# Two-layer decoder on one core: ScalarE copies the last turned group of each half in stages 1 and 3, and the row statistics move to the ends of halves

## What is computed

```python
x = x + _L0_attn_ref(_layernorm(x), qk, ov)                       # one causal head
x = x + _L0_xattn_ref(_layernorm(x), ctx, ctx, mask, Wq, bq, ...) # 16 heads of 16, mask, softmax
x = x + _L0_ffn_ref(_layernorm(x), w_router, b_router, w1, ...)   # relu FFN, top 4 of 16 blocks
x = x + _L1_attn_ref(_layernorm(x), w_qkv, b_qkv, w_o, b_o)       # 16 heads of 16, adds its input
x = x + _L1_xattn_ref(_layernorm(x), ctx, ctx, itok, ...)         # 16 heads, windows of 64, rotary
x = x + _L1_ffn_ref(_layernorm(x), gate_weight, w_gate, ...)      # top 2 of 8 experts + shared
```

## Time and profile before

| | us |
|---|---|
| median of 3 runs | 920.52 (920.5 to 922.61) |
| the profiled execution | 918.35 |
| its span, first to last instruction | 916.4 |
| TensorE matmuls busy | 858.8 (94%) |
| VectorE busy | 540.7 (59%) |
| ScalarE busy | 418.9 (46%) |
| GpSimd busy | 234.0 (26%) |

### The profile page before, as it was taken

One profiled execution on the slowest core, in us unless ns is written; L12 is line 12 of the kernel. 1 busy time (PEld: TensorE's weight loads), 2 busy tenths in 40 slices (PEclk: granted clock), 3 DMA queues, 4 the chain that ended last, 5 costly groups with the idle time before them and its releaser, 6 DMA issues.

```text
span 916.4 us, 16762 instructions
## 1 busy us (share of the span) xinstructions
PE 858.8 (94%) x6400; PEld 702.6 (77%) x6400; DVE 540.7 (59%) x1363; ACT 418.9 (46%) x1218; POOL 234.0 (26%) x352
## 2 busy tenths in 40 slices
PE   4889999997999999999999999999989999999998
PEld 3777777665888788777777777777758888888887
DVE  3565767777333321577777766666655555555554
ACT  1345566565322223566665567666674212222211
POOL 2112112221232112223232656666500000000000
PEclk9999999999999999999999999999989999999999
DMA  9700000000000000000000100000000000000000
GB/s 338 302 1 19 19 13 13 13 24 5 20 12 24 12 12 11 2 2 1 1 2 1 59 13 13 22 15 2 2 1 1 12 1 13 12 13 12 12 13 11
DMA packets 10909, 24.61 MB, mean 27 GB/s; under 512 B 1488, under 2 KB 5840, under 8 KB 9680
## 3 DMA queue, kind: packets, MB, share of 16 engines
q1 hardware_dynamic: 10832, 23.55, 7.1%
HBM read 21.45 MB, written 2.10 MB: 26 GB/s over the span
## 4 chain that ended last, share of the span: by engine, by line
PE 77%; ACT 10%; DVE 10%; issue 1%; DMA 1%; SPq 0%; POOL 0%; DVEq 0%; POOLq 0%; ACTq 0%
PE sc L556 15%; PE pj L293 9%; PE pj L286 7%; ACT pr L1115 7%; PE ov L455 6%; PE pj L379 6%; PE sc L442 6%; PE sc L368 6%; PE ov L566 4%; PE pj L566 4%; PE ov L390 3%; PE pj L280 3%; PE sc L363 3%; DVE pT L792 2%; PE ov L293 2%; DVE xn L736 1%
## 5 line engine op out<-in xcount | busy, mean ns | idle before, releaser
L1115 ACT ACTIVATE pr<-sc,mx 128x128 f32<-128x128 f32 x768 | 216.7, 414 | 116.9 <-DVE mx L785 116.9
L785 DVE TENSOR_REDUCE mx<-sc 128x4 f32<-128x512 f32 x192 | 119.2, 683 | 56.5 <-PE sc L368 56.5
L379 PE MATMUL pj<-idn,pr 128*128 128x128 f32 x768 | 120.9, 281 | 20.8 <-ACT pr L1115 13.2
L792 DVE COPY pT<-pj 128x512 f32<-128x512 f32 x160 | 109.5, 686 | 33.5 <-PE pj L379 31.8
L379 PEld LDWEIGHTS pj<-idn,pr 128*128 128x128 f32 x768 | 88.1, 142 | 49.6 <-issue 20.4
L1257 POOL TENSOR_SCALAR ve<-mv 128x2 f32<-128x2 f32 x40 | 8.9, 221 | 377.1 <-DVE mv L731 377.1
L1153 ACT ACTIVATE sh<-sc 128x256 f32<-128x256 f32 x80 | 30.7, 384 | 155.6 <-PE sc L556 155.6
L1133 ACT ACTIVATE hT<-sc,vecs 128x256 f32<-128x256 f32 x64 | 30.4, 475 | 95.4 <-PE sc L442 95.4
L556 PE MATMUL sc<-xnT,W 128*128 128x256 f32 x256 | 66.4, 382 | 0.0
L556 PE MATMUL sc<-xnT,Wup 128*128 128x256 f32 x256 | 65.7, 379 | 0.0
L442 PE MATMUL sc<-xnT,W 128*128 128x256 f32 x256 | 64.1, 380 | 0.0
(11 more groups left out here) (170 smaller groups left out, 1550.0 us busy)
## 6 DMA issues: line engine op xcount, KB each, us to landing
cT<-in_ctxT SPq DMA_DIRECT2D x16, 256.0 KB, 3.1
W<-in_w SPq DMA_DIRECT2D x2, 1024.0 KB, 13.6
cT<-in_ctx SPq DMA_DIRECT2D x8, 256.0 KB, 2.7
out_x<-X SPq DMA_DIRECT2D x8, 256.0 KB, 2.0
X<-in_x SPq DMA_DIRECT2D x1, 1792.0 KB, 8.1
rws<-in_rows SPq DMA_DIRECT2D x1, 1064.0 KB, 12.0
hT<-in_tokk SPq DMA_DIRECT2D x1, 1024.0 KB, 10.4
Wx<-in_w_x SPq DMA_DIRECT2D x1, 1024.0 KB, 16.4
```

Source lines behind the costliest of these rows:

```text
L379: last = tr(bank[b][:, i * S:(i + 1) * S], pr[n % 4][:, i, :], idn[:])
L785: v.tensor_reduce(mx[n % 4][:], four(b), AX.X, ALU.max, negate=True).then_inc(mx_done, 1)
L792: v.tensor_copy(pT[n % 4][:], four(b)).then_inc(drained[b], 1)
L1115: last = a(pr[n % 4][:, i, :], bank[b][:, i * S:(i + 1) * S], ACT.Exp, bias=mx[n % 4][:, i:i + 1])
```

## The change

Four things are edited. `ACT_TURNS` gives groups 3 and 7 of stages 1 and 3 to ScalarE. On VectorE `alone0` and `alone1` go to the end of their half, behind `part1` and `part3`; `alone0` now holds `x_norm(U + 2)`, `alone1` holds `x_stats(U + 3)`, one half earlier than `x_stats(U + 2)` at the start of the next unit, so the loops begin at -3. The router's choice and the experts' weights go from `alone1` to `part2`. GpSimd's `x_inverse(U + 2)` goes from `part1` to the head of `part0`. TensorE's list of instructions is the same.

```diff
-        ACT_TURNS = {1: (), 3: (), 4: (1, 3, 5, 7)}
+        ACT_TURNS = {1: (3, 7), 3: (3, 7), 4: (1, 3, 5, 7)}
...
                 dense(U, 2 * j)
-                if f not in ATT:
-                    (alone0, alone1)[j](U)
                 (part0, part2)[j](U)
                 if f in ATT:
                     copy_probs(U, 4 * j)
-                    (alone0, alone1)[j](U)
                 dense(U, 2 * j + 1)
                 (part1, part3)[j](U)
+                (alone0, alone1)[j](U)
...
+                if stage(U + 1) == 2:
+                    router_choice(U + 1)
+                if stage(U + 1) == 5:
+                    weights(U + 1)
...
             def alone0(U):
-                if stage(U + 2) is not None:
-                    x_stats(U + 2)
+                if stage(U + 2) in (0, 1, 2, 3, 5):
+                    x_norm(U + 2)
                 if stage(U) == 2:
                     ctx_stats(U % PAIRS)
...
             def alone1(U):
-                if stage(U + 2) in (0, 1, 2, 3, 5):
-                    x_norm(U + 2)
-                if stage(U + 1) == 2:
-                    router_choice(U + 1)
-                if stage(U + 1) == 5:
-                    weights(U + 1)
+                if stage(U + 3) is not None:
+                    x_stats(U + 3)
...
             def part0(U):
+                if stage(U + 2) is not None:
+                    x_inverse(U + 2)
...
             def part1(U):
                 if stage(U + 1) == 4:
                     rotate(U + 1, 0)
-                if stage(U + 2) is not None:
-                    x_inverse(U + 2)
...
-            for U in range(-2, UNITS + 2):
+            for U in range(-3, UNITS + 2):
```

## The result

The changed kernel takes 911.9 us (median; 908.83 to 913.04 over 4 runs) against 920.82 beside it (920.5 to 922.61). The ratio is 0.9894, with a 95% interval of 0.9867 to 0.9921: about 1% faster (the ratio is estimated from all runs of both, not from the two medians). 912.2 had been forecast. The profiled execution took 911.74, with a span of 909.9 us; before it was 918.35 with 916.4.

The account below looks back on a forecast made before the run. TensorE, 77% of the last chain, was taken as the bound, so only holes in its work could be won. Terms 3.6 + 0.6 + 2.2 + 2.8 + 0.8 + 0.2 - 1.9 = 8.3 us gave a 912.2 us median, range 908.5 to 917.5.

Parts of the forecast that it names:

- (f): Stage 2, units of fold and center: statistics delay the residual TensorE waits for, 0.94 us each, a loss of 1.9 us.
- (c): ScalarE's 32 copies fit where it idles: 0 us, bound 0 to 0.1 per copy, up to 3.
- (g): Start: xn of pair 2 escapes GpSimd's memsets, 2.2 us, plus 0.6 of clock: 2.8 us, bounds 1.0 and 3.6.
- (a): Second halves of stage 1: x_norm leaves between copies 4 and 5, 3.6 us; first unit of stage 3, 0.6 us.
- (b): First halves of stages 1 and 3: statistics leave, x_norm at the end is hidden: no gain or loss.
- (d): Second halves end with statistics of three units ahead, 0.94 us, hidden: 0 us, thinnest cover 0.27 us in stage 3.
- (e): Stage 4: without statistics ahead of it the value step starts some 0.27 us earlier, eight times: 2.2 us.
- (h): Last unit of stage 1: copy 5 no longer behind x_norm and router's choice, 0.8 us; end of stage 4, 0.2 us.
- given back: Many-head stages: ScalarE's exponentials set the unit's pace, so freed time is lost; 919.2 us, no change; 12%.
- The slower one: Second halves of stages 1, 3, 4: statistics in front of the maxima delay the chain, 932.9 us in full; 6%.
- "More": TensorE's lower clock near 220 and 675 us goes with the holes ahead: two us, 910.2 or less; 10%.

Follow-up runs that it names:

- the second experiment, experiment 2: Changed kernel with the old ACT_TURNS table, so VectorE makes all copies of stages 1 and 3: 912.01 us, ratio 0.9918 to the kernel before.
- experiment 4: Changed kernel with statistics issued before VectorE's wait for the last fold or center in those two units: 906.7 us, ratio 0.9858 to the kernel before.
- experiment 7: Changed kernel with the weight chain at the end of stage 4 (unit 39) issued behind the norm's last group: 911.85 us, ratio 0.9902 to the kernel before.
- experiment 3: Changed kernel with four extra row statistics ahead of the maxima after each second half of stage 3: 915.19 us, ratio 0.9932 to the kernel before.

## Why the prediction was right, point by point

The sum was 8.3 us against the profiled execution; the spans differ by 6.5. That the median came within 0.3 us of the forecast is partly luck. The sum was 1.8 us too high, (f) alone by 1.6, and the medians differ by 2.4 us more than the profiled executions do. The ends of the range, 908.5 and 917.5, are not what the bounds of (c) and (g) give, 911.4 and 917.0; the median lies inside these too. The mechanisms held at the large places. (f) left a part out, and the end of stage 4 was seen wrongly.

The terms by the two traces, as TensorE's instructions come ahead from stage to stage:

| term | foretold | measured |
|---|---|---|
| (a) second halves of stage 1, first unit of stage 3 | 3.6 + 0.6 | 3.6 + 0.6 |
| (b), (c), (d) first halves, copies, statistics in stage 3 | 0 | 0.0 |
| (e) stage 4 | 2.2 | 1.9 |
| (f) two residuals of stage 2 | -1.9 | -3.5 |
| (g) start | 2.8 | 2.3 |
| (h) end of stage 1, end of stage 4 | 0.8 + 0.2 | 1.9 - 0.3 |
| sum | 8.3 | 6.5 |

(a) is exact to 0.1, and the second experiment confirms its cause: the halves become 8.25 us with the new order and the old table. (c) was rightly taken as nothing for ScalarE. But the prediction's "the thinnest cover, 0.27" for (d) was right only because the table is part of the change; with VectorE making the copies the cover is gone, and 1.5 us go (experiment 2).

(e): the eight units gave 0.24 each, not 0.27. The longest wait of the kind is 0.33 where it was 0.56, and in all it fell from 4.5 us to 2.7.

(f) is the term that was mis-sized. The 0.94 us of each block came as foretold, 0.93 and 0.92. What the step left out is that a longer wait can be followed by matmuls at 1.2 GHz, which took 1.68 us more at the first of the two places. The prediction spoke of the clock only as something to win.

(g) came out near its number by a sum of three things. The hole between the first and the second scores shrank by 2.31 (7.94 to 5.63), as foretold (2.2). The stretch behind it, 6.54 us before with the clock at 0.52 in part, took 5.46: 1.08 for the 0.6 foretold. The hole's size is one execution's: in the other six traces with this order it is 4.65 to 5.86. And the first scores came 1.06 us later than in the trace of before, since the first `xn` did (14.61 against 13.97) and the turn behind it ran slower (1.08 against 0.63). The change doesn't touch those: experiment 4, with the old order, has 14.82 and 1.09 for them. That TensorE turned at 21.06 and not at 20.2 is due to the projections ahead of it, which took 3.15 us.

Of the small `nmx` the step had said that the memsets hold it. It ended at 19.49 (19.4 foretold) but took only 0.26 us against 0.17, since the softmax had come 1.4 us later and the long memsets were over at 19.20. So its end near 19.4 was luck. That an instruction as small as that can be held for the whole of one of GpSimd's is true all the same, by other rows: `tops` (128x8) took 1.17 us and not 0.17 in stage 2 of the kernel before.

(h): at the end of stage 1 the wait of 0.46 is gone, and by the traces 1.0 us is won there, for 0.8 foretold. The stretch at the lower clock lies at another place in it (0.72 on average from 219 to 225 before, 0.72 from 214 to 220 now), and what that is worth was not separated. The other 0.85 of the 1.9 is the wait for `nm` in the first unit of stage 2, which the prediction had not named: the three traces with the old order have this wait of 0.7 us, the seven with the new one don't. At the end of stage 4 the turn of the changed kernel was late by 1.37 us, which the prediction had not seen. It spoke of a gain of 0.2 there and didn't ask what `weights` would hold in its new place ahead of copy 4. From that turn's neighbours on it still wins 0.34 (experiment 7); what was lost lies ahead, in the stretch at the lower clock.

The rivals: the freed time was not "given back" in the many-head stages (first halves 9.72 in both). The slower one names a real mechanism: past its cover the third stage pays one for one (experiment 3). The change stays 0.27 us short of using up VectorE's idle time, and 0.6 short of costing TensorE anything. "More" did not come: the stretches at the lower clock near 220 and 675 us stayed. The one from 24 to 26 us is gone, and one in stage 2 has come. The matmuls before 21 us are slow in both (last section).

## What to carry to other kernels

Taking work off an engine that is not waited for gives nothing, here 32 copies for 0 us; moving one 0.65 us step out from between two copies that a full ring of buffers hangs on gave 0.6 us a unit. Price a moved block by the idle time in front of whoever waits next, and then look one wait further: the next wait may take up a part of the lateness, 0.33 us here, or take back most of a gain, as with the 1.37 that was worth 0.34. After such a change, look for the few units where the moved block meets a different neighbour (here two of eight in one stage). Together with a like wait in a stage that the change left as it was, setting these right brought as much again as the whole change.

## What the runs showed of the hardware

- Behind a wait of TensorE of about 2.0 to 2.4 us in a dense stretch the granted clock fell to its lower level in 7 cases of 10; behind 1.1 to 1.5 us at the same places in none of 10. So single executions of one kernel can differ by the 1.7 us that it cost each time. A wait's length alone does not tell, though: near 221 us in the kernel before, where TensorE had waited 1.02 and 0.89 us one after the other, the clock fell too.
- At the start of the changed kernel the matmuls are as slow as at the lower level, eight scores in 1.91 us against 1.13 later, while the record of the granted clock says 1.00:

```profile
16.37 1.91 PE L321 MATMUL sc<-xnT,qT 128*128 128x128 f32 x8
...
22.00 1.13 PE L321 MATMUL sc<-xnT,qT 128*128 128x128 f32 x8 [0.34 <-ACT qT L1099]
```

```profile
16.00:18.00 2.00, 2.00 (x11) 2.00 (x10) 0.50 (x6) 0.60 (x1) 1.54 (x3) 1.00 0.98 394
```

In the kernel before the same stretch reads 0.50. So at the start the durations tell more than the clock column; what slowed them here stays open.
- ScalarE copies a turned group in 0.60 us, VectorE in 0.69.
- An instruction of VectorE can be held until one of GpSimd beside it ends, and small ones are held as long as large ones. Of the two of `xn` (0.4 us each) one took 1.90 us beside the memsets. `tops`, a copy of 128x8, took 1.17 instead of 0.17 beside a GpSimd instruction of 1.26; `nm`, 128x32, 1.23 instead of 0.18 (at 266.76 in the kernel before).
